# An extra wait on GpSimd before every second gather of the expert stage

## The reference

```
x = layernorm(x + attention(x))        # 16 heads of 8, causal, with output projection
logits = x @ Wg.T                      # 8 experts
w, idx = top_k(softmax(logits), 2);  w = w / sum(w)
h = silu(x @ W1[e].T) * (x @ W3[e].T)  # hidden width 352, for the two chosen experts e
y = sum over the two experts of w * (h @ W2[e].T)
out = layernorm(x + y)
```

## Time and profile before

| what | value |
|---|---|
| median of 3 runs | 970.11 us (959.4 to 973.43) |
| the profiled execution | 967.69 us, span 965.9 us, granted clock 0.912 |
| busy: PE, PEld, DVE, ACT, POOL | 83%, 62%, 60%, 50%, 57% of the span |
| expert tiles, first to last `act_a` | 492.1 to 909.9 us |
| gathers and scatters | 136 of each |

### The profile page before, as it was taken

How to read it: one execution, slowest core, us unless ns; L and a number is a source line. 1 busy time by engine, 2 the same in 40 slices (tenths; PEclk the granted TensorE clock), 3 DMA queues, 4 the chain that set the end, 5 groups by cost and what they waited for, 6 DMA issues and landing times.

```text
span 965.9 us, 22691 instructions
## 1 busy us (share of the span) xinstructions
PE 797.9 (83%) x7734; PEld 598.2 (62%) x7734; DVE 584.0 (60%) x1478; ACT 483.0 (50%) x1150; POOL 553.0 (57%) x719
## 2 busy tenths in 40 slices
PE   8899999999999999871458887878778778868876
PEld 6566666666666666541257876867677777757822
DVE  4778888888888888619924433344343344434446
ACT  1577777777777777747523222222222232222337
POOL 6356666666666666653056666656566566656652
PEclk8999999999999999975669899899899897999979
DMA  5344444444434443105911111111111111111196
GB/s 173 131 138 138 138 138 138 136 138 134 136 124 141 136 131 125 46 7 193 165 37 39 45 42 45 42 44 42 43 42 45 42 40 42 45 42 40 42 309 220
DMA packets 71597, 93.99 MB, mean 97 GB/s; under 512 B 10336, under 2 KB 50016, under 8 KB 71232
## 3 DMA queue, kind: packets, MB, share of 16 engines
q1 hardware_dynamic: 62640, 74.21, 25.0%
q0 software_dynamic: 8704, 17.98, 7.3%
q10 hardware_dynamic: 144, 0.35, 0.1%
HBM read 56.26 MB, written 34.14 MB: 94 GB/s over the span
## 4 chain that ended last, share of the span: by engine, by line
PE 21%; another core or an unknown queue 11%; issue 8%; DVE 5%; ACT 3%; DMA 1%; POOL 1%; ACTq 0%; DVEq 0%; SPq 0%; POOLq 0%
PE ps_xy L1264 6%; PE ps_a L1246 5%; PE ps_b L1246 4%; PE ps_h L1278 2%; PE ps_xy L1269 2%; DVE z_stats L1217 1%; ACT rows_out L1159 1%; DVE h L1201 1%; ACT act_a L1155 1%; ACT x_high L1163 1%; DVE offset L1223 1%; DVE x_low L1193 1%; DVE z_mv L1228 1%; POOL picked_rows L1136 1%
## 5 line engine op out<-in xcount | busy, mean ns | idle before, releaser
L378 DVE TENSOR_REDUCE neg_max<-ps_s 128x6 f32<-128x768 f32 x256 | 240.5, 950 | 33.4 <-PE ps_s L586 25.2
L242 POOL TENSOR_SCALAR_AFFINE_SELECT probs<-probs 128x512 f32<-128x512 f32 x256 | 162.9, 637 | 154.7 <-ACT probs L313 154.1
L313 ACT ACTIVATE probs<-ps_st 128x768 f32<-128x768 f32 x256 | 207.7, 811 | 65.7 <-PE ps_st L600 64.8
L1155 ACT ACTIVATE act_a<-ps_a 128x352 f32<-128x352 f32 x136 | 63.6, 467 | 305.0 <-DMA dense<-shift_t 142.8
L1136 POOL DMA_INDIRECT picked_rows<-rows_out,pairs x136 | 134.2, 986 | 127.9 <-ACT rows_out L1159 102.3
L1129 POOL DMA_INDIRECT xg<-x_rows,pairs x136 | 131.8, 969 | 79.8 <-issue 40.2
L1193 DVE TENSOR_TENSOR x_low<-ps_xy,x_high 128x128 fp32r<-128x128 f32 x136 | 39.1, 287 | 195.5 <-ACT x_high L1163 113.7
L1264 PE MATMUL ps_xy<-w_sb,h_t 128*128 (+1 forms) x816 | 128.4, 299 | 0.9 <-issue 0.9
L580 PE MATMUL ps_s<-dense 32*128 32x256 f32 (+1 forms) x1024 | 113.6, 297 | 13.6 <-ACT probs L313 9.9
L1264 PEld LDWEIGHTS ps_xy<-w_sb,h_t 128*128 128x128 f32 (+1 forms) x816 | 120.1, 212 | 6.1 <-issue 5.9
L580 PEld LDWEIGHTS ps_s<-dense 32*128 32x128 f32 x1024 | 77.6, 183 | 69.9 <-issue 59.7
(11 more groups left out here) (188 smaller groups left out, 1412.1 us busy)
## 6 DMA issues: line engine op xcount, KB each, us to landing
dense_rows<-split SPq DMA_DIRECT2D x32, 512.0 KB, 2.7
dense<-dense_rows SPq DMA_DIRECT2D x64, 256.0 KB
dense<-dense_rows SPq DMA_DIRECT2D x64, 128.0 KB
pick<-picked_rows SPq DMA_DIRECT2D x16, 512.0 KB, 5.4
x_rows<-y_all SPq DMA_DIRECT2D x8, 520.0 KB, 8.5
xt_sb<-xt SPq DMA_DIRECT2D x32, 128.0 KB, 2.3
x_sb<-x SPq DMA_DIRECT2D x32, 128.0 KB, 2.5
out<-normal SPq DMA_DIRECT2D x16, 256.0 KB
```

What stands on the lines that cost most here:

```text
L242: last = pool.affine_select(out=part, in_=part, compare_op=ALU.is_ge, fill=0.0, base=0, pattern=[[0, 2 * BLOCKS], [1, P]], channel_multipl ...
L313: act.activation(probs[:, g, 2 * half:2 * half + 2, 0:L + P], ps_st[:, :, 0:L + P], ACT.Exp, scale=float(HEAD_DIM) ** -0.5).then_inc(exp_d ...
L378: v.tensor_reduce(out=neg_max[:, h * GROUP + j:h * GROUP + j + 2, :], in_=ps_s[:, j:j + 2, 0:L + P].rearrange("p b (c t) -> p b c t", t=P) ...
```

## The change

Before gather s with s even, GpSimd waits for the first signal of iteration s - 12 + 5, that is, of the iteration in which TensorE makes the result that scatter s-12 sends, the scatter next on GpSimd's queue. `front` does nothing for iterations below -3, so the waits are there from s = 4 on, at 66 of the 136 gathers. Nothing else changes: the same instructions and the same DMAs in the same order.

```diff
@@ experts_and_combine
     NAMED = 17
+    PAUSE_EACH = 2
@@ gpsimd
             for s in range(n + LEAD):
                 if s < n:
                     wait(pool, share_ready, s - ROWS_IN)
+                    if s % PAUSE_EACH == 0:
+                        front(pool, s - LEAD + BEHIND)
                     pool.indirect_dma_start(
                         out=xg[:, s % ROWS_IN, :], out_offset=None, in_=x1_rows,
                         in_offset=bass.IndirectOffsetOnAxis(ap=pairs[:, s, 0:1], axis=0),
```

## The result

The changed kernel took 959.79 us (median of 20 runs, 953.65 to 970.58), the kernel before on the same chip 964.67 (20 runs). The ratio is 0.9937, 95% interval 0.9916 to 0.9959: faster by 0.6%, some 6 us (the two medians differ by 4.9), where 24 were forecast. The profiled execution of the changed kernel took 953.65 us, the quickest of its runs, with a span of 951.8; that of the kernel before, 967.69 us, was 3 us above its median. So the two traces lie 14 us apart and show more than the medians do.

A forecast was written before the change was run, and what follows sets the result against it. GpSimd, 2.57 us per tile, was nearest bound, with TensorE's signals stuck during its unbroken issuing. A gain of 24 us, between 36 - 9 = 27 and 19, gave 967.7 - 24 = 943.7, said as 945; range 918 to 982.

The forecast's parts named there:

- What bounds the kernel: Expert tiles: GpSimd nearest bound, 2.57 of 3.09 us per tile; TensorE's signals get stuck while GpSimd issues without a break.
- all prompt: Rival: shorter GpSimd runs hold no signal, GpSimd's 2.57 us per tile set the pace, 908 us; chance 0.08.
- Draining frees the signals: At a paused gather: once GpSimd's issued work has drained, all stuck TensorE signals come together, 1.97 us after a scatter's start.
- The restart: At a paused gather: GpSimd goes on at 720.63, just after the `act_a` of 720.61, 0.70 us beyond its gap.
- the sum: Four-tile GpSimd cycle: mean gain 1.3 us times 28, 36 us, less 9 for later scatters; 24 taken between 27 and 19.
- And doesn't wait again in this cycle: GpSimd's four-tile cycle: after pausing at the first gather, no further wait; 0.70 us replaces 2.21, a gain of 1.5.
- The list of signs: Changed trace: scatter waits from 102 to about 50 us, `act_a` waits down some 25, gather waits near 10, clock about 0.9.
- The replay: GpSimd's cycle replayed, signals stuck from 4.4 us into a run: three-tile drains, 2.98 us per tile against 3.12, 19 us gained.
- The base: Whole kernel before the change: profiled execution 967.7 us, 2.4 under the median of 970.1, from which 24 was taken.
- The pauses don't bite: Rival: draining GpSimd frees no signal early, or signals have always come; pauses cost 0 to 9 us, 968 to 979; chance 0.22.
- The clock rival: Longer TensorE stalls drop its clock, 28 cycles x 1.6 = 45 us more, about 1013 us; chance 0.15.
- the runs of six: GpSimd issuing six instructions back to back, scatter and gather three times, before its first gap; forecast to be gone.

The follow-up runs named there:

- the swapped kernel: The changed kernel with its two waits before the gather in the other order, TensorE's signal first, then `share_ready`: 944.47 us, 0.9771 of the kernel before.

## Why the prediction was wrong

**What bounds the kernel** was right: TensorE's signals come late while GpSimd issues indirect DMAs back to back. With GpSimd at one indirect DMA per tile they are prompt. This is needed for the lateness, but not enough, as the occasion without it shows. What the lateness costs in all can be read there: 883 us for 965. The rival "all prompt" had 908.

**Draining frees the signals** was right: 2.04 us after the last scatter's start, and all that were stuck together, at 25 of 26 pauses in the change and at all of the swapped kernel's.

**The restart** was the first step that failed. "GpSimd goes on at 720.63" put the gather 0.02 us after the `act_a` of 720.61, which the same signal frees. It starts 0.72 us after it, behind a wait instruction of its own that the kernel before doesn't have. A pause was so put at 1.0 us with its gap (0.70 beyond it) and took 1.7 (46.9 us in 28): 46.9 less 28 is 19 us, as much as the gain fell short by. I had costed a wait that is met, correctly, at nothing (0.9998), and not one that isn't. With 0.24 in its place the change is worth 21 us, 0.977, near the 24 forecast; but that kernel pauses 55 times and has another cycle, so this does not confirm the sum.

**"And doesn't wait again in this cycle"** was the second. The sum took the cycle of four tiles as given and removed 1.1 to 1.5 us of idle time from it. But the wait of 2.35 us at a scatter stays in the changed kernel: after a pause GpSimd issues seven instructions back to back, and signals are stuck again. Of 102 us of scatter waits 47 are left. The list of signs had "about 50", but the sum had not: it left one wait of 0.70 us in half of the cycles, some 10 us. The pauses cost 47 us, where 28 of them were put at 20 us without their gaps and 28 with them. So the waits were moved rather than removed; 9 us are gone. The replay saw that the cycle might change. It had drains 9.8 and 8.1 us apart, 2.98 us per tile, where the change has 11.0 and 7.9 in the stretch shown, 3.15. It also took signals as stuck from 4.4 us into a run, while the one due at 716.99 was stuck 3.5 us into the run of 713.50. That 2.98 equals the swapped kernel's steady 5.97/2 is luck: its cycle is two tiles, not three.

**The base.** The profiled execution (967.7) and the three runs (970.1) lay above the median of 20 runs, 964.7. This made the miss look smaller, not larger: 24 us off 964.7 would have been 941, 19 us under the measured 959.8, and the base, 4 us too high, hid part of it. What was mis-sized is the gain, 24 us for 5 to 6.

**Rivals.** "The pauses don't bite" gave a time close to the measured one (968 for 960), and its reason is refuted: they bite 28 times and free the signals. The clock rival did not come: 0.89 in the stage for 0.90, and 0.98 with the waits swapped, where long stalls are fewer. The Trainium skill's rule in DMA: Bandwidth & Descriptors, rules for kernel authors (issue early, wait late), would have had the change slower; TensorE waits 10.5 us for gathers as before, so on this lead it costs nothing, and pausing the gathers gained. What was shown wrong in the list of signs: `act_a`'s waits didn't fall by 25 us (276 for 276), and the runs of six went, but runs of seven took their place. Gather waits at 10 us, the clock at 0.9 and a stage under 418 us were right.

## What to carry to other kernels

When an engine waits for a signal whose sender has, by the trace, long finished, look at what GpSimd is issuing at that moment: two indirect DMAs per tile, one each 1.28 us without a break, held TensorE's signals by up to 6 us, one per tile didn't. If they can't be thinned out or made plain, try letting GpSimd stop before it has to, on a signal that it will need next, which gained 0.5 to 2.7% here. Price a wait that is really waited on by the restart behind it, which here was 0.24 or 0.72 us by nothing but the order in which two waits were written, and ask what the engine does after the pause: here it ran longer than before and lost again what it had won. Measure such a kernel on more than one occasion: the same program took 883 and 965 us.

## What the hardware showed beyond expectation

- A signal of TensorE can reach the engines that wait for it 6 us after the matmul's end (7 us for a second signal in the change, 13.7 us behind 19 gathers in a row), while a signal of ScalarE passes in 0.25 us. In this kernel it was seen only with indirect DMAs that GpSimd issues back to back. It was not seen with about the same bytes on SyncE, with plain gathers beside one indirect scatter per tile, or with 0.95 us fills in their place. What holds the signal was not found.
- Most late signals come about when an indirect DMA's data has moved, 1.85 to 2.1 us after the start of a scatter or 2.0 to 2.45 after that of a gather: of the late `act_a` that ScalarE stood waiting for, 47 of 53 in the kernel before, 34 of 50 in the change and 37 of 40 with two gathers per tile. The others fit neither distance, and nothing here says why.
- Two waits before one GpSimd DMA: where the signal really waited for was that of the wait written first, the DMA followed 0.24 us after it, and 0.72 us where it was that of the second. One that was already met cost nothing.
- All of the lateness was absent on one occasion, for every kernel run then: 882.84 us for 965 (8.5%). What differed wasn't found.
